# Attention: a product of 256 columns without a use ahead of every fourth score

## The reference, cut to what matters

```python
def _L1_attn_ref(x, w_attn, w_proj):
    qkv = x @ w_attn
    q, k, v = jnp.split(qkv, 3, axis=2)
    q = q.reshape(Bc, Tc, H, HD).transpose(0, 2, 1, 3)   # k and v alike
    att = jnp.einsum('bhqd,bhkd->bhqk', q, k) * (1.0 / math.sqrt(HD))
    causal = jnp.tril(jnp.ones((Tc, Tc), dtype=bool))
    att = jnp.where(causal[None, None], att, -jnp.inf)
    att = jax.nn.softmax(att, axis=-1)
    y = jnp.einsum('bhqk,bhkd->bhqd', att, v)
    y = y.transpose(0, 2, 1, 3).reshape(Bc, Tc, Dc)
    return y @ w_proj
```

## Time and profile before

| | |
|---|---|
| time before, median of 3 runs | 1819.66 us (1818.97 to 1830.32) |
| the profiled execution | 1823.95 us |
| its span, first to last instruction | 1822.1 us |
| TensorE busy | 1664.9 us (91%) |
| mean granted TensorE clock | 0.943 |
| attention, first score to last weighted sum and projection | 1478.6 to about 1654 us of the span |

### The profile page before, as it was taken

How to read it: one execution, slowest core, us unless ns; L and a number is a source line. 1 busy time by engine, 2 the same in 40 slices (tenths; PEclk the granted TensorE clock), 3 DMA queues, 4 the chain that set the end, 5 groups by cost and what they waited for, 6 DMA issues and landing times. The chain is left out here.

```text
span 1822.1 us, 29135 instructions
## 1 busy us (share of the span) xinstructions
PE 1664.9 (91%) x9564; PEld 1229.5 (67%) x9564; DVE 1176.0 (65%) x2682; ACT 898.6 (49%) x2394; POOL 576.0 (32%) x877
## 2 busy tenths in 40 slices
PE   3889999999999999999999999998869799996897
PEld 2457778787787877778777787777745455554575
DVE  4468687776877778677686877867354534444345
ACT  1556656666575665756657566664221023341121
POOL 1415344252442424434253342523110012121303
PEclk9889999999999999999999999999679978777898
DMA  1010110101101010010101101001011080000413
GB/s 67 12 38 7 34 40 4 38 7 34 29 14 39 7 35 16 25 40 7 35 13 28 40 7 34 7 17 17 1 58 35 18 336 1 1 1 1 151 53 93
DMA packets 120722, 65.61 MB, mean 36 GB/s; under 512 B 91392, under 2 KB 111744, under 8 KB 120448
## 3 DMA queue, kind: packets, MB, share of 16 engines
q1 hardware_dynamic: 119040, 59.56, 11.7%
q0 software_dynamic: 1536, 4.20, 0.7%
HBM read 46.16 MB, written 17.56 MB: 35 GB/s over the span
## 5 line engine op out<-in xcount | busy, mean ns | idle before, releaser
L852 DVE SCALAR_TENSOR_TENSOR dr_acc<-dr_raw,dr_wh,dr_acc 128x512 f32<-128x512 f32 x384 | 307.3, 814 | 57.8 <-ACT dr_acc L717 56.0
L1071 PE MATMUL dr_pp<-xnT,dr_wh 128*128 128x512 f32 x512 | 247.2, 617 | 6.0 <-DMA dr_wh<-in_w_head 5.6
L676 POOL TENSOR_TENSOR dr_dT<-dr_dT,cst 128x512 f32<-128x512 f32 x64 | 88.4, 1382 | 252.3 <-DVE dr_dT L886 252.3
L662 POOL TENSOR_TENSOR dr_gm<-cst,dr_hs 128x512 f32<-128x512 f32 x64 | 76.7, 1209 | 259.6 <-DVE dr_hs L846 132.0
L1071 PEld LDWEIGHTS dr_pp<-xnT,dr_wh 128*128 128x128 f32 x512 | 93.8, 195 | 92.1 <-issue 73.6
L1146 PEld LDWEIGHTS dr_pI<-dr_Y,dr_nl 128*64 128x64 f32 (+1 forms) x1536 | 129.4, 160 | 33.8 <-issue 26.6
L1161 PEld LDWEIGHTS dr_pI<-dr_V,dr_X 128*64 128x64 f32 (+1 forms) x1536 | 130.1, 160 | 28.9 <-issue 21.0
L1146 PE MATMUL dr_pI<-dr_Y,dr_nl 128*64 128x64 f32 (+1 forms) x1536 | 138.4, 245 | 4.7 <-DMA dr_Y<-dr_blocks_y 3.1
L1161 PE MATMUL dr_pI<-dr_V,dr_X 128*64 128x64 f32 (+1 forms) x1536 | 139.6, 247 | 1.0 <-DVE dr_V L976 0.8
L1103 PE MATMUL dr_pp<-dr_wh,xnT 128*128 128x256 f32 x512 | 124.5, 387 | 14.8 <-ACT dr_acc L717 14.8
L716 ACT ACTIVATE dr_raw<-dr_pp 128x512 f32<-128x512 f32 x128 | 76.2, 595 | 113.3 <-PE dr_pp L1071 90.3
(11 more groups left out here) (260 smaller groups left out, 3600.8 us busy)
## 6 DMA issues: line engine op xcount, KB each, us to landing
dr_wh<-in_w_head SPq DMA_DIRECT2D x16, 776.0 KB, 4.5
ex_w<-in_moe SPq DMA_DIRECT2D x18, 608.0 KB, 11.9
dr_wo<-in_w_out SPq DMA_DIRECT2D x16, 256.0 KB, 4.7
dr_sorted_x<-ex_zero SPq DMA_DIRECT2D x1, 3968.0 KB, 26.9
dr_sorted_y<-so_xt SPq DMA_DIRECT2D x31, 128.0 KB, 1.7
m_w<-in_moe SPq DMA_DIRECT2D x8, 384.0 KB, 3.1
so_xt<-dr_sorted_x SPq DMA_DIRECT2D x3, 1024.0 KB, 9.2
dr_blocks_l<-dr_nl SPq DMA_DIRECT2D x128, 16.0 KB, 1.7
```

What stands on the lines that cost most here:

```text
L662: pool.tensor_tensor(gm[p][:], over(k.c(C_LE), 1, U), over(hs[s][:, G_, units(c)], 2, P), ALU.mult).then_inc(s_gm[p], 1)
L676: pool.tensor_tensor(d, d, over(k.c(C_LE), 1, U), ALU.mult).then_inc(s_am, 1)
L852: dve.scalar_tensor_tensor(acc[q][:], raw[q][:, w:w + S], wh[at.ps][:, col:col + 1], acc[q][:], ALU.mult, ALU.add).then_inc(done[q], 1)
L1071: mm = pe.matmul(flat(ps), wh[at.ps][:, w0:w0 + P], k.xnT[:, kt, b * S:(b + 1) * S], start=(kt == 0), stop=(kt == KT - 1))
```

## The change

A new function issues products whose result nobody reads. In `score`, ahead of scores 0, 4, 8 and 12 of each group and behind the wait for the bank, it issues one: the identity as weights on all 128 rows, the first 256 columns of `cst` moving, into the first 256 columns of the bank that the score then overwrites. The product signals no semaphore.

```diff
+def idle_products(k, pe, bank, count, columns=512):
+
+    for _ in range(count):
+        pe.matmul(bank[:, 0:columns], k.c(C_IDENT), k.cst[:, 0:columns], start=True, stop=True)
...
                 ps = unit_free("s", g, i)
+                if i % 4 == 0:
+                    idle_products(k, pe, ps, 1, 256)
                 rows = slice(SLOT * r, SLOT * (r + 1))
```

## The result

The changed kernel takes 1840.43 us (median of 20 runs, 1823.37 to 1850.75) against 1822.53 us before (20 runs, 1815.77 to 1830.32): a ratio of 1.009, 95% interval 1.0071 to 1.0109. It is 17.9 us slower. By the ratio that is just within the 1% that the prediction called no change, though above the 1837.9 us that it worked out from 1819.66; it is 7 us above the range, and on the other side of the forecast of 1817.5.

The account below looks back on a forecast made before the run. TensorE, busy 91%, was taken as the engine to look at, its clock falling in attention. Gain 12.65 + 4.2 = 16.9 us less cost 14.7 gave net -2.2, so 1817.5 us from 1819.66; range 1802 to 1833.

Parts of the forecast that it names:

- What bounds the kernel, and where: Attention, 176 of 1822 us: TensorE busy 91% of the span; its granted clock tells good steps from bad.
- What a steady full clock is worth: Attention's eight steps all at full clock like step 2, the 17.57 us one: 25.3 us gained at most.
- The price of a product: Ahead of scores 0, 4, 8, 12: 0.46 us each at full clock, 0.92 at half; 14.7 us with score 4's hidden.
- the lost overlap of row groups: Full-array products at scores 8 and 12 stand alone: 0.6 us more each, 9.6 over 8 steps; forecast took nothing.
- I take half of the excess as kept: Attention's steps: the products recover half of the 25.3 us lost to slow clock, 12.65 us.
- the 4.2 us for slow stretches that end sooner: In steps that still fall, products at scores 8 and 12 recover a third of the other half, 4.2 us.
- B: Rival: attention's clock falls as before in nearly every step; +18.4 us, 1838 us; chance 0.13.
- C: Rival: clock held in every attention step, each product at its 0.46 us; -10.6 us, 1809 us; chance 0.22.
- D: Rival: clock held, products at scores 4, 8 and 12 hidden under VectorE; -21.6 us, 1798 us; chance 0.10.
- E: Rival: as A, with row-group overlap lost at scores 8 and 12; +9.6 us on A, 1827 us; chance 0.15.
- A: Likeliest case: half of attention's slow-clock excess recovered; 1817.5 us, own range 1810 to 1825; chance 0.40.
- The rule on idle gaps: Skill's rule for TensorE's clock: products that close no idle gap change nothing, giving B's time, 1838 us.

Follow-up runs that it names:

- e10_rows32_mid: Against the changed kernel: products of 512 columns on the score's own 32 rows, ahead of scores 4 to 11 alone; 1801.7 us, 0.9893 of the kernel before.
- e1_in_gap: Against the changed kernel: the same 32 products ahead of scores 2, 6, 10 and 14 instead of 0, 4, 8 and 12; 1814.07 us.
- e12_plus_s6: The changed kernel plus one more full-array product of 256 columns ahead of score 6 of each group; 1814.21 us.
- e4_one512: Against the changed kernel: one full-array product of 512 columns ahead of score 6 of each group, none elsewhere; 1810.2 us.
- e6_s5_s7: Against the changed kernel: full-array products of 256 columns ahead of scores 5 and 7 alone, behind the score's wait; 1818.7 us.

## Why the prediction was wrong

**What bounds the kernel, and where.** Right. Nothing outside attention moved by more than the profiles differ among themselves, and the clock is what tells a good step from a bad one.

**What a steady full clock is worth.** About right, a little low. e10_rows32_mid gains 21.2 us by the medians of its chip (1822.92 to 1801.7) although its steps at full clock still last 1.1 us over 17.57, some 8 us in all; that makes about 29, by estimate, for the "upper bound" of 25.3. One term of the bound was too high: the projections were taken out of steps 6 and 7 at 3.60 us, but from first score to first score step 6 is only 2.95 us shorter than step 5 in e1_in_gap (16.62 and 19.57) and in e10_rows32_mid (15.70 and 18.65), which makes 24.0 of the 25.3. The profiled execution of before had a long way to attention (1478.6 us, at the late end of the 1470.3 to 1479.0) and so a short attention for its total; the prediction supposed the opposite. That this is the reason is argued, not shown, since other executions' steps were not recorded.

**The price of a product.** Mis-sized, but little. Predicted was 1.84 us for four at full clock, 1.38 with score 4's hidden; e1_in_gap's four cost 2.0, and the change's own full-clock step 1 lasts 19.18 us where about 19 were forecast. VectorE's idle time ahead of score 0 is 1.72 us in step 2, for a forecast of 1.5. For a step that falls, 2.76 less 0.46 hidden, 2.3 us, was predicted; measured were 2.6 (23.90 against 21.30 us, steps with 10.24 us of slow clock) and 3.0 (25.48 against 22.46). The term left at nothing in the forecast, the lost overlap of row groups, is there: at half clock 1.8 of the 3.0 us, at full clock about 0.1 us a product.

**Does it hold the clock?** Here is the step that failed: "I take half of the excess as kept", 12.65 us, and with it the 4.2 us for slow stretches that end sooner. Neither came. One step of eight was held, as many as before; no run shows why that one, and it can be called luck as step 2's was. The slow stretches of the eight steps add up to 81.9 us in the profile after, for 71.7 before, so the clock gave back nothing of the 16.9 us forecast and the price of the products stood alone. The reason against it stood in the same paragraph: nothing is added in the more than 4 us between scores 4 and 8, where four of the six falls lay. The evidence was read rightly and then discounted on the strength of one step that had passed. e1_in_gap and e12_plus_s6 show that it was this lack: the same products two scores later, or one more ahead of score 6, hold every step and take 26 us off. Nor did the products at scores 8 and 12 end the slow stretch sooner: slow stretches last 6.8 to 17.1 us after the change, 6.8 to 13.7 before. The one product of e4_one512, ahead of score 6, went with stretches of 3.4 us in most of its steps that fell.

**The rivals.** B, the clock falls as before, with 18.4 us more and 1838, is what happened: 1840.43, 17.9 more. It got a chance of 0.13 and the range was drawn to leave it out. B's sum is nearly right in total although its price per step (2.3 for 2.6 to 3.0) was low. C, the clock held throughout with each product at its price, is what e1_in_gap shows: 1809 us, from 0.46 us a product, against 1814 measured with 0.5. D, products hidden under VectorE, showed nowhere among the kernels with four full-array products a step, whose steps with projections last 18.75 us or more at full clock. E's lost overlap was real, but as a part of B and not of A.

**The rule on idle gaps.** The Trainium skill, "TensorE: Matmul & The Clock Gate", section "Why this matters for your kernels", which ties a falling clock to idle gaps between bursts, gave B's time, and the time came out so, but not for its reason: between the first score and the fall TensorE idles 0.3 us at most in the steps shown (busy 5.36 of 5.64 and 7.17 of 7.46 us after, 4.43 of 4.43 in step 4 before), and e1_in_gap holds the clock by adding work where there was no gap to close.

## What to carry to other kernels

In this kernel products without a use helped the clock where they stood in the stretch in which it falls, and not ahead of it: find the falls in each step first, put the product there, look for the stretch that falls next, and expect that a product there need not be enough in every step (e6_s5_s7). In a stretch of row-packed products, fill the rows of the score itself and do not stop all four row groups: eight products of 512 columns on 32 rows cost 1.1 us a step, four of 256 columns on 128 rows 2.0. When a row says that nothing is added at the place that decides, let it decide the forecast, and not one step that got by.

## What was not expected of the hardware

In step 4 before, the clock fell to half with TensorE busy for 4.43 of 4.43 us, and after the change it stayed there for 13.65 us with TensorE busy for all of them. The work in this place is packed products of 32 rows, and yet more products of 32 rows in the places of e1_in_gap helped to hold the clock (falls in four steps of eight, 1818.5 us), less than those of 128 rows (none, 1814.07 us). Full-array products of 32 columns among packed products cost no less time over the kernel than those of 256 (1845.87 against 1840.43 us; the intervals of the ratios just touch). And falls can repeat at one place: steps 4 and 5 of the changed kernel fall 7.46 us after the first score in each, and last 23.90 and 23.88 us. What sets that place is not shown.
